# QKV and FF1 in three passes on split operands, with all engine orders rewritten, in an eight-layer block kernel

## The reference

```python
q = x @ Wq + bq ; k = x @ Wk + bk ; v = x @ Wv + bv        # 128 x 128 each
Q = elu(q) + 1 ; K = elu(k) + 1
KV = sum over tokens of K * v ; Ksum = sum over tokens of K  # one number per feature and sequence
Z = 1 / (Q * Ksum + 1e-6)
V = Q * KV * Z
attn = gelu(V @ Wo + bo)
x = layernorm(attn + x) * ln1_s + ln1_b
h = gelu(x @ Wf1 + bf1)                                     # 128 -> 512
ff = gelu(h @ Wf2 + bf2)                                    # 512 -> 128
x = layernorm(ff + x) * ln2_s + ln2_b
```

## Time and profile before

| | |
|---|---|
| Time, median of 3 runs | 550.27 us (549.25 to 550.69) |
| The profiled execution: its own time | 552.4 us |
| Its span, first to last instruction | 550.4 us |
| TensorE busy | 524.2 us (95%), mean granted clock 0.991 |
| VectorE busy | 434.3 us (79%) |
| ScalarE busy | 380.9 us (69%) |
| GpSimd busy | 246.8 us (45%) |

### The profile page before, as it was taken

How to read it: one execution, slowest core, us unless ns; L and a number is a source line. 1 busy time by engine, 2 the same in 40 slices (tenths; PEclk the granted TensorE clock), 3 DMA queues, 4 the chain that set the end, 5 groups by cost and what they waited for, 6 DMA issues and landing times.

```text
span 550.4 us, 7866 instructions
## 1 busy us (share of the span) xinstructions
PE 524.2 (95%) x1892; PEld 295.7 (54%) x1892; DVE 434.3 (79%) x1659; ACT 380.9 (69%) x532; POOL 246.8 (45%) x281
## 2 busy tenths in 40 slices
PE   3789999999999999999999999999988999999996
PEld 2345555555555555555555555555544345766663
DVE  5758888888888888888788888888885858888854
ACT  2757788887877888878777888887765545564642
POOL 2234454444554544455545544545442343555451
PEclk9989999999999999999999999999988999999999
DMA  8200010001000000100010010001000000000000
GB/s 249 72 0 17 5 38 2 14 5 38 14 5 19 19 14 5 38 14 5 7 31 14 5 38 14 0 5 38 0 2 0 0 2 1 19 1 21 0 20 20
DMA packets 15910, 11.21 MB, mean 20 GB/s; under 512 B 8189, under 2 KB 13693, under 8 KB 15893
## 3 DMA queue, kind: packets, MB, share of 16 engines
q1 hardware_dynamic: 15316, 10.42, 6.9%
q10 hardware_dynamic: 576, 0.60, 0.3%
HBM read 9.96 MB, written 1.05 MB: 20 GB/s over the span
## 4 chain that ended last, share of the span: by engine, by line
PE 87%; DVE 5%; issue 3%; POOL 2%; DMA 1%; ACT 0%; SPq 0%; DVEq 0%; POOLq 0%
PE bank L369 19%; PE bank L360 15%; PE bank L284 12%; PE bank L357 6%; PE bank L384 5%; PE bank L320 4%; PE bank L317 4%; PE bank L466 3%; PE bank L468 3%; PE bank L329 2%; PE bank L323 2%; PE bank L469 2%; PE bank L470 2%; PE bank L506 2%; PE bank L525 2%
## 5 line engine op out<-in xcount | busy, mean ns | idle before, releaser
L369 PE MATMUL bank<-hid,wf 128*128 128x512 f32 x256 | 125.6, 593 | 0.0
L360 PE MATMUL bank<-x,wf 128*128 128x512 f32 x192 | 94.1, 599 | 0.0
L720 POOL TENSOR_TENSOR rsD<-veD,c_half 128x4 f32<-128x4 f32 x32 | 38.4, 1200 | 121.7 <-DVE veD L809 121.7
L632 ACT ACTIVATE hid<-bank,vbf 128x512 f32<-128x512 f32 x128 | 80.9, 688 | 6.8 <-PE bank L360 3.9
L369 PEld LDWEIGHTS bank<-hid,wf 128*128 128x128 f32 x256 | 45.6, 189 | 46.5 <-ACT hid L632 27.2
L733 POOL TENSOR_TENSOR y<-g,xs 128x512 f32<-128x512 f32 x32 | 40.7, 1273 | 39.2 <-ACT g L638 39.2
L681 ACT ACTIVATE sg<-bank 128x512 f32<-128x512 f32 x40 | 23.9, 597 | 46.8 <-PE bank L470 35.0
L360 PEld LDWEIGHTS bank<-x,wf 128*128 128x128 f32 x192 | 37.2, 194 | 33.4 <-issue 22.7
L786 POOL TENSOR_TENSOR sc_lo<-sc,sc_hi 128x512 fp32r<-128x512 f32 x28 | 36.4, 1301 | 39.6 <-ACT sc_hi L689 36.2
L796 DVE BATCH_NORM_STATS2 stB<-bank 128x6 f32<-128x128 f32 x128 | 28.5, 285 | 31.9 <-PE bank L284 31.9
L720 POOL TENSOR_TENSOR rsB<-veB,c_half 128x4 f32<-128x4 f32 x32 | 32.6, 1020 | 42.3 <-DVE veB L809 42.3
(11 more groups left out here) (148 smaller groups left out, 1100.4 us busy)
## 6 DMA issues: line engine op xcount, KB each, us to landing
wf<-in_w_f SPq DMA_DIRECT2D x16, 256.0 KB, 2.7
wu<-in_w_unit SPq DMA_DIRECT2D x10, 192.0 KB
wqkv<-in_w_qkv SPq DMA_DIRECT2D x7, 192.0 KB, 2.3
x<-in_x SPq DMA_DIRECT2D x4, 256.0 KB, 6.3
out<-ot SPq DMA_DIRECT2D x4, 256.0 KB, 2.9
wo<-in_w_o SPq DMA_DIRECT2D x8, 64.0 KB, 1.8
wmod<-in_w_mod ACTq DMA_DIRECT2D x1, 384.0 KB, 4.1
vln<-in_v_ln SPq DMA_DIRECT2D x16, 1.0 KB, 1.7
```

The costliest lines, as they stand in the source:

```text
L360: mm = nc.tensor.matmul(ps_ff[j][:], wf1[:, j * P:(j + 1) * P], x2[(c - 2) % CH][:], start=True, stop=True)
L369: mm = nc.tensor.matmul(ps_f0[:], wf2[:, j, :], hid[:, j, :], start=(j == 0), stop=(j == FJ - 1))
L632: nc.scalar.activation(hid[:, j, :], ps_ff[j][:], ACT.Gelu_apprx_tanh, bias=vbf1[:, j:j + 1]).then_inc(h_ready, 1)
L720: nc.gpsimd.tensor_tensor(rs[buf(k, n)][:], ve[buf(k, n)][:], c_half[:], ALU.pow).then_inc(rstd_ready[k], 1)
```

## The change

Every Q, K, V and FF1 product becomes three fp32r passes on split operands (`high`, two passes, and `low`, the third). For these the program makes more data:

- x of the next layer is written twice by ScalarE from the same bank, as xs and, rounded, as xs_hi; GpSimd makes xs_lo.
- FF1's input is written twice by VectorE, x2_hi and x2, each now as one instruction of 512 columns; GpSimd makes x2_lo.
- Weights are rounded on ScalarE and their remainders made on GpSimd, once a layer: V's in the first slot of a layer, FF1's in the second, K's and Q's of the next layer in the fourth.

K and V now use one bank (ps_kv), V after K has been read. FF1's last quarter keeps the bank that was K's. The last norm's transpose back goes to Q's bank (`last_bank`), the first norm's to ps_y. GpSimd's power and VectorE's normalisation of the norms B and D are each done in two halves. Some buffers of the expert stage now share memory with those of the layers; the expert stage is otherwise the same. The DMA of FF1's weights moves ahead of the biases, and va is loaded in two pieces. The order on every engine is rewritten. The core of the diff:

```diff
@@ -225,24 +236,25 @@
             def layer_loads(l, first):
 
                 if not first:
-                    sp.wait_ge(v_mm, CH * l)
+                    sp.wait_ge(wkq_lo_ready, l)
+                    sp.wait_ge(wv_lo_ready, l)
                     sp.dma_start(wqkv[:], w_qkv[l]).then_inc(ld["wqkv"], 16)
+                    sp.wait_ge(wf_lo_ready, l)
+                sp.dma_start(wf1[:], w_f1[l]).then_inc(ld["wf1"], 16)
+                if not first:
+                    sp.wait_ge(elu_q, CH * l)
+                    sp.wait_ge(k_ready, CH * l)
+                    sp.dma_start(va[:, 0:2], v_a[l, :, 0:2]).then_inc(ld["va"], 16)
...
+                nc.tensor.matmul(bank[:], w_hi, a_hi[:], start=True, stop=False)
+                nc.tensor.matmul(bank[:], w_lo, a_hi[:], start=False, stop=False)
+
+            def low(bank, w_hi, a_lo):
+
+                return nc.tensor.matmul(bank[:], w_hi, a_lo[:], start=False, stop=True)
 
...
+                if has(a):
+                    pe.wait_ge(x_hi_ready, a + 1)
+                    pe.wait_ge(x_ready, a + 1)
+                    if c == 0:
+                        pe.wait_ge(wkq_lo_ready, l + 1)
+                    if has(a - 1):
+                        pe.wait_ge(elu_q, a)
+                    high(ps_q, wqkv_hi[:, q_w], wqkv_lo[:, q_w], xs_hi[c])
                 if has(f):
-                    ff1(0)
-                    ff1(1)
-                    ff1(2)
+                    pe.wait_ge(normed["B"], HB * f + 2)
+                    transposes(ps_y, xh["B"], to_fm["B"], last_halves)
+                if has(a):
+                    pe.wait_ge(x_lo_ready, a + 1)
+                    low(ps_q, wqkv_hi[:, q_w], xs_lo[c]).then_inc(q_mm, 1)
+                    if has(a - 1):
+                        pe.wait_ge(kv_ready, a)
+                    high(ps_kv, wqkv_hi[:, k_w], wqkv_lo[:, k_w], xs_hi[c])
...
+                    if (c - 2) % CH == 0:
+                        pe.wait_ge(wf_lo_ready, l + 1 if c > 1 else l)
+                    ff1_high(0)
+                if has(d):
+                    pe.wait_ge(y2_ready, d + 1)
+                    if not has(a):
+                        pe.wait_ge(x_ready, d + CH)
+                    transposes(ps_d, y2, to_tm["D"])
...
+                if has(f):
+                    pe.wait_ge(x2_lo_ready, f + 1)
+                    ff1_low(0)
+                    ff1_low(1)
+                    pe.wait_ge(x2_ready, f + 1)
+                    ff1_high(2)
+                    ff1_low(2)
+                    if has(f - 1):
+                        pe.wait_ge(h_ready, 4 * f)
+                    ff1_high(3)
+                    ff1_low(3)
...
+                if has(a):
+                    pe.wait_ge(k_ready, a + 1)
+                    if c == 0:
+                        pe.wait_ge(wv_lo_ready, l + 1)
+                    high(ps_kv, wqkv_hi[:, v_w], wqkv_lo[:, v_w], xs_hi[c])
+                    low(ps_kv, wqkv_hi[:, v_w], xs_lo[c]).then_inc(v_mm, 1)
+                if has(b):
+                    pe.wait_ge(normed["B"], HB * b + 1)
+                    transposes(ps_y, xh["B"], None, first_halves)
...
-                        if (c - 3) % CH == 0:
-                            act.wait_ge(ld["vln2"], 4 * d + 16)
-                        nc.scalar.activation(xs[(c - 3) % CH][:], ps_d[:], ACT.Identity,
-                                             bias=vln2[:, 1:2], scale=vln2[:, 0:1]).then_inc(x_ready, 1)
+                if c == 0 and has(a) and not (isinstance(s, int) and s == 0):
+                    act.wait_ge(v_mm, a)
+                    act.wait_ge(ld["wqkv"], 16 * l + 16)
+                    nc.scalar.activation(wqkv_hi[:, 2 * P:], wqkv[:, 2 * P:], ACT.Copy).then_inc(wv_hi_ready, 1)
+                if c == 1 and has(a):
+                    if has(f):
+                        act.wait_ge(ff1_mm, 4 * f + 4)
+                    act.wait_ge(ld["wf1"], 16 * l + 16)
+                    nc.scalar.activation(wf1_hi[:], wf1[:], ACT.Copy).then_inc(wf_hi_ready, 1)
+                if c == 3 and has(a + 1):
+                    act.wait_ge(ld["wqkv"], 16 * l + 32)
+                    nc.scalar.activation(wqkv_hi[:, 0:2 * P], wqkv[:, 0:2 * P], ACT.Copy).then_inc(wkq_hi_ready, 1)
+                if has(d):
...
+            def rstd_half(k, n, h):
+                pool.wait_ge(var_ready[k], n + 1)
+                j = slice(h * T // 2, (h + 1) * T // 2)
+                nc.gpsimd.tensor_tensor(rs[k][:, j], ve[k][:, j], c_half[:, j], ALU.pow).then_inc(rstd_ready[k], 1)
+
+            def rest(lo, x, hi):
+                return nc.gpsimd.tensor_tensor(lo, x, hi.bitcast(F32), ALU.subtract)
+
+            def x_lo(n, c):
+                pool.wait_ge(x_ready, n + 1)
+                pool.wait_ge(x_hi_ready, n + 1)
+                rest(xs_lo[c][:], xs[c][:], xs_hi[c][:]).then_inc(x_lo_ready, 1)
...
```

More of the change, by code:

```diff
@@ L53, in adaln_block @@
         xs = [sb(f"xs{c}", [P, G]) for c in range(CH)]
+        xs_hi = [sb(f"xs_hi{c}", [P, G], F32R) for c in range(CH)]
+        xs_lo = [sb(f"xs_lo{c}", [P, G], F32R) for c in range(CH)]
         x2 = [sb(f"x2_{c}", [P, G]) for c in range(CH)]
+        x2_hi, x2_lo = sb("x2_hi", [P, G], F32R), sb("x2_lo", [P, G], F32R)
         vt = [sb(f"vt{c}", [P, G]) for c in range(CH)]
@@ L187, in run, with last_bank @@
                 extra[place]()
+        def last_bank(a):
+            return ps_q if has(a) else ps_d
         def splits(i):
@@ L364, in ff2, with ff1_high, ff1_low @@
+                def ff1(j):
+                    w = slice(j * P, (j + 1) * P)
+                    return wf1_hi[:, w], wf1_lo[:, w], ps_ff[j]
+                def ff1_high(j):
+                    w_hi, w_lo, bank = ff1(j)
+                    high(bank, w_hi, w_lo, x2_hi)
+                def ff1_low(j):
+                    w_hi, w_lo, bank = ff1(j)
+                    low(bank, w_hi, x2_lo).then_inc(ff1_mm, 1)
                 def ff2(j):
@@ L542, in unit_0 @@
                 up(0)
-            slot(NI, 0, LAYERS, {"start": lambda: zf_to_tm(0)})
+            slot(NI, 0, LAYERS, {"after the last sum": lambda: zf_to_tm(0)})
             norm_to_fm(0)
@@ L741, in slot, with rest_of_x_lo @@
                     qh.then_inc(q_ready, 1)
-                run(extra, "end")
-                if has(b):
-                    rstd("B", b)
-            slots(pool, slot)
-            slot(NI, 0, LAYERS, {"end": lambda: rstd("F", 0)})
+                if c == 0 and has(a) and not (isinstance(s, int) and s == 0):
+                    wv_lo(l)
+                if c == 1 and has(a):
+                    pool.wait_ge(wf_hi_ready, l + 1)
+                    rest(wf1_lo[:], wf1[:], wf1_hi[:]).then_inc(wf_lo_ready, 1)
+                if c == 3 and has(a + 1):
+                    wkq_lo(l + 1)
+                run(extra, "middle")
+                if has(b):
+                    for h in range(HB):
+                        rstd_half("B", b, h)
+                if has(d) and has(d + CH):
+                    x_lo(d + CH, (c - 3) % CH)
+                if has(f):
+                    pool.wait_ge(g2_ready, f + 1)
+                    nc.gpsimd.tensor_tensor(y2[:], g2[:], x2[(c - 2) % CH][:], ALU.add).then_inc(y2_ready, 1)
+                if has(b):
+                    pool.wait_ge(x2_ready, b + 1)
+                    pool.wait_ge(x2_hi_ready, b + 1)
+                    rest(x2_lo[:], x2[(c - 1) % CH][:], x2_hi[:]).then_inc(x2_lo_ready, 1)
+                if has(f) and has(f + 1):
+                    rstd_half("D", f, 0)
+                if has(a):
+                    pool.wait_ge(g1_ready, a + 1)
+                    nc.gpsimd.tensor_tensor(y1[:], g1[:], xs[c][:], ALU.add).then_inc(y1_ready, 1)
+                if has(f) and has(f + 1):
+                    rstd_half("D", f, 1)
+            def rest_of_x_lo():
+                for c in range(1, CH):
+                    x_lo(c, c)
+            slots(pool, slot, {"middle": rest_of_x_lo})
+            slot(NI, 0, LAYERS, {"middle": lambda: rstd("F", 0)})
             slot(NI + 1, 1, LAYERS)
-            pool.wait_ge(g2_ready, NI)
-            nc.gpsimd.tensor_tensor(y2[:], g2[:], x2[CH - 1][:], ALU.add).then_inc(y2_ready, 1)
             def split_weights(u):
@@ L775, in _ @@
                 if i == U + 2:
-                    rstd("D", NI - 1)
+                    for h in range(HB):
+                        rstd_half("D", NI - 1, h)
                 if n < CH:
@@ L920, in slot @@
                                                    op0=ALU.mult, op1=ALU.mult).then_inc(nck_ready, 1)
+                if has(b):
+                    nc.vector.tensor_scalar(x2[(c - 1) % CH][:], ps_y[:], vln1[:, 0:1], vln1[:, 1:2],
+                                            ALU.mult, ALU.add).then_inc(x2_ready, 1)
+                if has(a):
+                    dve.wait_ge(nck_ready, a + 1)
+                    dve.wait_ge(dd_ready, a + 1)
+                    for h in range(HB):
```

(6 more changed lines are left out.)

305 lines of the change are left out of this document (147 added, 158 removed).

## The result

The changed kernel takes 593.38 us (median, 591.73 to 594.05), the kernel before beside it on the same chip 549.77: a ratio of 1.078, 95% interval 1.074 to 1.081. I had said 546, from 535 to 577: wrong in direction and outside the range.

What follows compares the result with a forecast made beforehand. TensorE was taken to bound the layer loop, 12.26 us a slot (one chunk group at four stages); VectorE would then set 12.0. 29 x (12.26 - 12.0) = 7.5 off, 3 on at the start: 546 us, range 535 to 577.

Steps and rivals of the forecast that it cites:

- Passes, products, start: TensorE passes at 0.227 us each; VectorE's x2_hi and x2 at 0.72 each; +3 us before the first Q.
- Half power: GpSimd's two-column power in the norms: 0.61 us, between bounds 0.20 and 1.02; VectorE waits 0.64 for it.
- The circle of ScalarE and TensorE: From g2 through ScalarE's table loads, g1 and hid to TensorE's FF2 and back: a floor of 11.8 us a slot.
- The rival of an unshortened power: GpSimd's power costs 1.02 for two columns as for four: slot 12.8, 569 us; chance 0.08.
- The lock on v: Rival: GpSimd's x2_lo gets in between VectorE's v halves, holding the second: 1.04 a slot, 576 us; chance 0.22.
- Meetings at half price: VectorE's small operations stand beside GpSimd's at three places: 0.67 a slot at full price, half taken, 0.34.
- expected gain: TensorE in the layer loop: three passes for each of 7 products take 1.3 us off a slot, to 10.95.

Runs made afterwards that it cites:

- number 10: Changed kernel with x2 written by ScalarE behind dd instead of by VectorE, plus the edits of number 6 and 8: 572.35 us, ratio 1.040.
- number 9: Changed kernel with edits 1, number 6 and 8 together, and dif as a three-operand instruction: 566.13 us, ratio 1.030.
- 1: Changed kernel with GpSimd's x2_lo additionally waiting for the v of its slot: 573.74 us, ratio 1.041.
- number 6: Changed kernel with zf's transposes behind FF1's products in the slot behind the last layer: 590.42 us, ratio 1.072.
- number 5: Changed kernel with the powers of norms B and D computed whole again, normalisations still in halves: 597.63 us, ratio 1.086.
- 8: Changed kernel with ScalarE's wait for the load of Wo's biases moved ahead of eq: 588.01 us, ratio 1.069.
- 12: Changed kernel's order without splitting: single float32 products, Q's and K's weights loaded apart from V's, plus number 6 and 8: 564.26 us, ratio 1.027.
- 13: Changed kernel with x2 written half by VectorE, half by ScalarE behind dd, plus 1, number 6 and 8: 573.14 us, ratio 1.041.

## Why the prediction was wrong, point by point

- **Passes, products, start.** Right. A pass has a pitch of 0.23 in the loop, x2_hi and x2 0.73 and 0.72 as forecast, the start cost 1.2 (I said 3, from 0 to 6).
- **Half power.** Right in effect: 0.67 where I took 0.61, and VectorE waits 0.66 where I had 0.64. The rival of an unshortened power (0.08) is out.
- **The circle of ScalarE and TensorE.** Right within 0.15: 11.8 forecast, 11.95 worked out from number 10 (12.61 less x2's 0.66); no run has the circle alone as its limit.
- **The lock on v: the step that failed.** The prediction had it as a rival with 0.22, since "the margin is 0.05 us, and either may win". It priced it at 1.04 a slot and 576 us. It costs 1.01 and occurs in all 32 slots; taking it out gives 19.6 us back. The price of the lock was right, the chance was not. The gap between v's two halves is there in every slot, GpSimd stands ready 0.16 after v's start, and the same sequence of lengths repeats in each slot, so the race fell the same way every time. I treated a margin as a coin although I had myself read a case from the trace: GpSimd getting in between mk and mq. The lock alone is not the miss, though: with it I had 576, and of the 47 us between 546 and 593.4 it is 19.6, the table load 5.4 and zf 3.0; the other 20 are in number 9 still, whose slot is 12.62 where I had 12.0.
- **Meetings at half price: the second step that failed.** Too low: dif at 0.5 and 0.6 in numbers 1 and 9 is the full price. In number 9, from 222 to 400 us, the meetings lengthen VectorE's rows by 0.77 a slot (the last norm's dif 0.44, the first norm's 0.23 on average, nck 0.10), where I took 0.34 and had 0.67 as the full price. VectorE's waits are 0.89 a slot where I had 0.64, since I put those for the transposes and for norm D's power at nothing. Together that is 0.68 more, about the 0.62. The Trainium skill, "SBUF — State Buffer", section "Who interferes with whom", says that a VectorE instruction with two SBUF inputs contends with a GpSimd instruction that reads SBUF; number 9 agrees, dif waits in both forms. The Trainium skill, "SBUF — State Buffer", in the same section, has the block last the whole instruction; here it ends 0.1 to 0.2 us before GpSimd's shown end.
- **Not seen at all: the table load behind a wait** (5.4 us). I counted ScalarE's instructions and not where the load stands when g1 has two waits.
- **Not seen at all: the tail.** I wrote nothing for the last slot; it costs 6.6 us, of which number 6 gives back 3.0 by the times and 4.6 by the trace. How much of it is zf's is open, since number 5 has a tail of 149.3 with zf's transposes in place.
- **Where the expected gain went.** The 1.3 us a slot of TensorE are real by its rows (21 passes at 0.23), but with 1, 6 and 8 mended the loop stays at 12.62, 11.3 us over before, since, as I read it, VectorE's row with x2_hi, dif at full price and a wait of 0.66 is longer than TensorE's was. The four runs 9, 10, 12 and 13 stand within 0.04 of each other in the slot (12.61 to 12.65), by my reading with three different limits: VectorE's row in 9, ScalarE's circle in 10 and 13, TensorE with gaps in 12. That they fall together so closely may be chance; a limit common to all four is not excluded. That VectorE's row is the limit in number 9 rests on its rows; the run that should have shown it (10) met another limit at once, so this last part is argued, not shown.

No version here beats the kernel before; the best with split operands is number 9, 3.0% slower.
